# Transposed rows, 512 wide value products, and two reorderings in a three-part transformer layer

## The reference, cut to what matters

```python
x = x + xattn(layernorm(x), ctx)       # x is 256 x 512, ctx 4096 x 512
x = x + ssd(layernorm(x))              # state space block
x = x + experts(layernorm(x))          # 32 routed experts, 6 for a token, and shared ones

# xattn: 16 heads over 4 key/value heads; keys: 4096 of ctx, then the 256 own ones
scores = einsum('blhd,bmhd->bhlm', q, k_full) * scale + mask   # mask: causal on the own keys
out = einsum('bhlm,bmhd->blhd', softmax(scores), v_full) ; out @ wo

# ssd, in 2 chunks of 128 tokens, 16 heads
A_cs = cumsum(dt * A)                                   # over the tokens of a chunk
Lmat = where(tril, exp(A_cs[l] - A_cs[s]), 0)
y = (C B^T * Lmat) @ (x dt) + C @ state * exp(A_cs) + x D
y = rms(y * silu(z)) * norm_weight @ W_out

# experts
s = sigmoid(x @ gate_w); combine = top 6 of s, normed to the sum 1
out = sum_e combine_e * (silu(x wg_e) * (x wu_e)) @ wd_e + shared
```

## Time and profile before

| what | value |
|---|---|
| runs (3) | median 1078.52 us, 1077.47 to 1078.64 |
| the profiled execution | 1078.46 us |
| its span, first to last instruction | 1076.5 us |
| mean granted PE clock | 0.995 |
| busy share PE, DVE, ACT, POOL | 98%, 70%, 52%, 13% |

### The profile page before, as it was taken

How to read it: one execution, slowest core, us unless ns; L and a number is a source line. 1 busy time by engine, 2 the same in 40 slices (tenths; PEclk the granted TensorE clock), 3 DMA queues, 4 the chain that set the end, 5 groups by cost and what they waited for, 6 DMA issues and landing times.

```text
span 1076.5 us, 17012 instructions
## 1 busy us (share of the span) xinstructions
PE 1055.8 (98%) x6685; PEld 939.5 (87%) x6685; DVE 748.7 (70%) x1634; ACT 555.5 (52%) x956; POOL 139.7 (13%) x142
## 2 busy tenths in 40 slices
PE   7999999999999999999999999999999899999998
PEld 6888888878999999999999999999777599999997
DVE  5856777559677777777777777777178667676675
ACT  4434433335766656666655666667035445445442
POOL 4644444330000000000000000004021000000000
PEclk9999999999999999999999999999999899999999
DMA  6758666597004220044002340013520285555550
GB/s 229 253 193 281 199 228 195 167 315 251 1 1 167 81 86 2 1 167 131 37 2 89 118 132 1 1 71 141 227 120 1 81 338 179 181 191 187 181 172 20
DMA packets 64159, 145.85 MB, mean 135 GB/s; under 512 B 3888, under 2 KB 42704, under 8 KB 62672
## 3 DMA queue, kind: packets, MB, share of 16 engines
q1 hardware_dynamic: 64080, 144.77, 39.1%
HBM read 108.55 MB, written 36.21 MB: 134 GB/s over the span
## 4 chain that ended last, share of the span: by engine, by line
PE 92%; DVE 4%; ACT 1%; issue 1%; DMA 0%; POOL 0%; POOLq 0%
PE bank L434 58%; PE bank L453 16%; PE bank L532 11%; PE bank L591 2%; PE bank L463 1%; DVE conv_acc L1026 1%; PE bank L717 1%; PE bank L561 1%; PE bank L604 1%; PE bank L674 1%; PE bank L488 0%; DVE conv_acc L1023 0%; DMA w_ctx_raw<-in_w_ctx 0%; ACT xc L1390 0%; PE bank L635 0%
## 5 line engine op out<-in xcount | busy, mean ns | idle before, releaser
L962 DVE TENSOR_TENSOR pT_lo<-bank,pT_hi 128x512 fp32r<-128x512 f32 x272 | 185.2, 690 | 122.8 <-ACT pT_hi L1357 122.7
L434 PE MATMUL bank<-pT_hi,vN 128*128 128x256 f32 (+1 forms) x1088 | 245.0, 288 | 0.0
L1357 ACT CAST pT_hi<-bank 128x512 fp32r<-128x512 f32 x272 | 159.3, 587 | 161.4 <-PE bank L532 157.0
L434 PEld LDWEIGHTS bank<-pT_hi,vN 128*128 128x128 f32 x1088 | 185.9, 189 | 6.9
L434 PE MATMUL bank<-kT,qT_hi 128*128 128x512 f32 (+2 forms) x576 | 188.5, 408 | 2.1 <-DVE scores L907 2.1
L907 DVE TENSOR_SCALAR_CACHE_REDUCE scores<-bank 128x512 f32<-128x512 f32 x256 | 169.3, 682 | 0.1
L532 PE MATMUL bank<-ident,scores 128*128 128x128 f32 x1072 | 161.4, 272 | 0.9 <-DVE pT_lo L962 0.9
L434 PE MATMUL bank<-fT_hi,e_hl 128*128 128x256 f32 x816 | 156.2, 284 | 0.0
L1328 ACT ACTIVATE scores<-scores,neg_max 128x1024 f32<-128x1024 f32 (+2 forms) x128 | 153.1, 1196 | 5.7 <-DVE neg_max L919 5.7
L434 PE MATMUL bank<-pT_lo,vN 128*128 128x256 f32 (+1 forms) x544 | 153.1, 281 | 0.0
L453 PE MATMUL bank<-w_ctx_hi,ctx_hl 128*128 128x512 f32 x512 | 145.9, 397 | 6.4 <-ACT ctx_hl L1237 6.4
(11 more groups left out here) (201 smaller groups left out, 1349.0 us busy)
## 6 DMA issues: line engine op xcount, KB each, us to landing
e_raw<-in_experts SPq DMA_DIRECT2D x51, 768.0 KB, 4.4
k_spill<-k_stage SPq DMA_DIRECT2D x16, 1024.0 KB, 4.5
v_spill<-v_stage SPq DMA_DIRECT2D x16, 1024.0 KB, 8.6
vN<-v_spill SPq DMA_DIRECT2D x16, 1024.0 KB, 5.2
kT<-k_spill SPq DMA_DIRECT2D x15, 1024.0 KB, 5.3
ctx_raw<-in_ctx SPq DMA_DIRECT2D x15, 512.0 KB, 4.3
w_raw<-in_w_qkv SPq DMA_DIRECT2D x6, 1024.0 KB, 5.1
wo_sb<-in_wo SPq DMA_DIRECT2D x4, 1024.0 KB, 8.6
```

The lines of the kernel that those rows point to most:

```text
L434: done = e.matmul(dst, lhs(a), rhs(w), start=first and m == 0, stop=last and m == 2)
L962: e.tensor_tensor(ring[1][:, :], bank[tb][:, :], ring[0][:, :], ALU.subtract).then_inc(p_lo, 1)
L1357: e.copy(ring[0][:, :], bank[tb][:, :]).then_inc(p_hi, 1)
```

## The change

The reciprocals are spread by two transposes of a broadcast column, straight from `rden`; `diag` goes. The two parts of `pT` stand in one tile, and for a key tile one 512 wide product has V_hi with both parts (V_hi x pT_lo sums in columns 256 to 511 of the bank), and one 256 wide has V_lo x pT_hi. At a head's end DVE copies the upper half, adds the lower, and then multiplies. The decay rows become transposes of a broadcast column of `cs`. `project_z(1, 0)` comes ahead of the triangle product. The second tile's logits follow `up(0)`, the turned `cw` follows `up(1)`, and `up` no longer waits for the plain copy `fT` of the second tile.

```diff
-        pT = [[reg.take(f"pT_hi{i}", [512], F32R), reg.take(f"pT_lo{i}", [512], F32R)] for i, reg in enumerate([region["pt"]] * 3 + [sp_])]
+        pT = [reg.take(f"pT{i}", [2, 512], F32R) for i, reg in enumerate([region["pt"]] * 3 + [sp_])]
...
-                    done = three(bank[5 + z][:, q0:L], lambda v: vN[:, v, kt, :], lambda p: ring[p][:, i * L + q0:(i + 1) * L],
-                                 kt == 0, kt == KTILES - 2)
+                    halves = bank[5 + z][:, :].rearrange("p (a q) -> p a q", a=2)
+                    e.matmul(halves[:, :, q0:L], vN[:, 0, kt, :], ring[:, :, i * L + q0:(i + 1) * L], start=kt == 0, stop=False)
+                    done = e.matmul(halves[:, 0, q0:L], vN[:, 1, kt, :], ring[:, 0, i * L + q0:(i + 1) * L], start=False, stop=kt == KTILES - 2)
...
             def spread_sums(h):
-                pe.wait_ge(inv, 4 * (h + 1))
+                pe.wait_ge(inv, 2 * (h + 1))
-                e.matmul(bank[b][:, 0:L], ones[:, :], diag[h % 2][:, :, :].rearrange("p a b -> p (a b)"), start=True, stop=True).then_inc(spread, 1)
+                for qt in range(2):
+                    done = e.transpose(bank[b][:, qt * P:(qt + 1) * P], rden[h % 2][:, qt, 0:1].to_broadcast([P, P]), ident[:, :])
+                done.then_inc(spread, 1)
...
+            project_z(1, 0)
             pe.wait_ge(dtc, 18)
             e.matmul(bank[5][:, 0:TT * MH], upto[:, :], dA_.rearrange("p t h -> p (t h)"), start=True, stop=True)
             e.matmul(bank[5][:, 64:64 + MH], ones[:, :], dtb[8][:, 0, :], start=True, stop=True).then_inc(dt_mm, 1)
-            project_z(1, 0)
...
             def decay_rows(tt, c, q, bank_sem, bank_count):
-                pe.wait_ge(dtc, 18)
+                pe.wait_ge(cs_done, 1)
-                    done = e.matmul(bank[b][:, i * P:(i + 1) * P], dtb[8][:, tt, h0 + i:h0 + i + 1].to_broadcast([P, P]), upto[:, :], start=True, stop=True)
+                    done = e.transpose(bank[b][:, i * P:(i + 1) * P], cs[:, tt, h0 + i:h0 + i + 1].to_broadcast([P, P]), ident[:, :])
...
-            route_logits(1)
             def up(j):
-                pe.wait_ge(fT_l, 4)
+                pe.wait_ge(fT_l, 3)
...
                 up(j)
                 if j == 0:
+                    route_logits(1)
+                if j == 1:
                     pe.wait_ge(topk, 18)
...
             def invert_sums(h):
-                for qt in range(2):
-                    e.tensor_scalar(diag[z][:, qt, :], ident[:, :], rden[z][:, qt, 0:1], None, ALU.mult).then_inc(inv, 1)
...
             def finish_head(h):
-                e.tensor_tensor(head_out[z][:, :], bank[5 + z][:, 0:L], rden_all[z][:, :], ALU.mult).then_inc(ho, 1)
+                e.tensor_copy(head_out[z][:, :], bank[5 + z][:, L:2 * L]).then_inc(ho_sum, 1)
+                dve.wait_ge(ho_sum, 2 * h + 1)
+                e.tensor_tensor(head_out[z][:, :], bank[5 + z][:, 0:L], head_out[z][:, :], ALU.add).then_inc(ho_sum, 1)
+                dve.wait_ge(ho_sum, 2 * h + 2)
+                e.tensor_tensor(head_out[z][:, :], head_out[z][:, :], rden_all[z][:, :], ALU.mult).then_inc(ho, 1)
```

More of the change, by code:

```diff
@@ L280, in build_program @@
         rden = [sp_.take(f"rden{i}", [2, 1]) for i in range(2)]
-        diag = [sp_.take(f"diag{i}", [2, P]) for i in range(2)]
         rden_all = [sp_.take(f"rden_all{i}", [2 * P]) for i in range(2)]
@@ L374, in build_program @@
         p_hi, p_lo, pv, inv, spread, rden_done = sem("p_hi"), sem("p_lo"), sem("pv"), sem("inv"), sem("spread"), sem("rden_done")
+        ho_sum = sem("ho_sum")
         ho, oT_hi, oT_lo = sem("ho"), sem("oT_hi"), sem("oT_lo")
@@ L924, in invert_sums @@
                 e.reduce_sum(den[z][:, :, 0], sums[z][:, :, :], AX).then_inc(inv, 1)
-                dve.wait_ge(inv, 4 * h + 1)
+                dve.wait_ge(inv, 2 * h + 1)
                 e.reciprocal(rden[z][:, :, 0], den[z][:, :, 0]).then_inc(inv, 1)
-                dve.wait_ge(inv, 4 * h + 2)
-                for qt in range(2):
-                    e.tensor_scalar(diag[z][:, qt, :], ident[:, :], rden[z][:, qt, 0:1], None, ALU.mult).then_inc(inv, 1)
             def finish_head(h):
@@ L961, in dve_program @@
                     tb, ring = (3, 4, 7)[n % 3], pT[n % NPT]
-                    e.tensor_tensor(ring[1][:, :], bank[tb][:, :], ring[0][:, :], ALU.subtract).then_inc(p_lo, 1)
+                    e.tensor_tensor(ring[:, 1, :], bank[tb][:, :], ring[:, 0, :], ALU.subtract).then_inc(p_lo, 1)
                     for s in plan.in_step[h, kk]:
@@ L1356, in act_program @@
                             act.wait_ge(v_out[slot], 16 * NBATCH // 2)
-                    e.copy(ring[0][:, :], bank[tb][:, :]).then_inc(p_hi, 1)
+                    e.copy(ring[:, 0, :], bank[tb][:, :]).then_inc(p_hi, 1)
                     for p in plan.parts_in_step[h, kk]:
```

## The result

The changed kernel took 1070.12 us (median of 4 runs, 1069.87 to 1071.55), the kernel before, run beside it, 1078.58 us. The ratio is 0.9921, 95% interval 0.9909 to 0.9933. The same kernel run again gave 1069.65 us, ratio 0.9921 (0.9908 to 0.9933). So 8.5 us went, where 6.85 were forecast.

What follows compares the result with a forecast made beforehand. TensorE (PE) bounds attention, VectorE (DVE) the state space stretch. Attention -8.7, state space -0.15, clock +1.2 and expert entry +0.8 sum to -6.85 us: 1078.5 to 1071.7 us, own range 1070.5 to 1073.4, whole range 1068.4 to 1075.0.

Steps and rivals of the forecast that it cites:

- The last pair: Attention, each head's last two key tiles, odd one masked for 128 queries: 0.69 to 0.583 us, 0.107 saved, 1.7 in all.
- the spread: Attention, denominators' rows: two transposes at 0.22 us replace a full-precision product at 0.43, saving 0.21 x 16 = 3.4 us.
- 512 x 0.007 = 3.6 us: Attention, wide value product: each of 512 key tiles saves 2 x 0.120 - 0.233 = 0.007 us of PE.
- rival B: Attention: the wide value product saves nothing, as equal columns suggest; 1075.3 us, chance 0.13.
- C: Attention: the wide value product runs at 0.227 us, like the context projection's products; 1068.6 us, chance 0.11.
- The missing diagonals give nothing: Last head of attention: dropping two diagonal builds on DVE gains 0, since pT_lo there waits for ACT's cast.
- Cost nothing: Attention, head's end on DVE: head_out 0.85 to 0.9 us later, absorbed in two to three steps; uncovered 14.4 us.
- at least 3.4 us of cover: Attention, head's end: PE uses the delayed pT_lo three steps later, steps taking 1.16 to 2.56 us.
- The hole: State space part: PE's 1.63 us softplus idling, filled by the z product, only moves to 806.8 to 808.4; worth nothing.
- The clock near 811: State space part: PE, thinned to 2.6 of 6.1 us, falls to half clock for some 7 us, costing 1.2 us.
- rival A: State space part: the clock holds because transposes keep PE busy enough; 1070.5 us, chance 0.24.
- Entry of the experts: Start of the expert part: reordered logits make tile 2 start at 862.55, not 861.8; 0.8 us lost, 0.45 at full clock.

## Why the prediction was right, and where not

- **Attention, forecast 8.7, measured 7.85.** The last pair (0.106 a head) and the spread (0.21 a head) came as worked out; between the landmarks each counts in 15 heads, 1.6 and 3.2 us. The mis-sized term is "512 x 0.007 = 3.6 us": by the steps it is 4.5 ns a tile, 2.3 us. The step that failed is the pricing of a 256 wide product at 0.120 us, and with it of a tile's saving, from pieces rounded to 0.01 us. The Trainium skill, "TensorE: Matmul & The Clock Gate", section "Back-to-back issue gap", has a formula for a single warm matmul, N/2.4 ns plus 2.5, from which an estimate of 2.5 ns a merged pair follows, 1.3 us. The measured 2.3 lies between that and the forecast. Neither rival B (nothing) nor C (13 ns) holds.
- **"The missing diagonals give nothing": wrong by 1.2 us.** In the last head pT_lo waited for DVE as well, and not for ACT's cast alone. Three steps of it are 1.23 us longer in the trace before than in the one after, and 1.57 longer with the diagonals back in the changed kernel.
- **The head's end, "Cost nothing": right where score chunks run beside it, for the wrong reason, and wrong in the last head.** The step that failed is "at least 3.4 us of cover". It followed the delay through pT_lo alone. What comes first is the score eviction behind pT_lo, whose bank PE wants: 0.4 us are left after the change, by an estimate 1.3 before it with the 0.9 that the change took. A delay begins to cost from there, not from 3.4. In the last head nothing covers it, and the longer end costs 0.55 us. So the sum for attention is 2.3 + 1.6 + 3.2 + 1.2 - 0.55 = 7.75 of the 7.85.
- **State space part: 0.14 us measured, 0.15 forecast.** The hole moved, as told: PE of the changed kernel waits 1.75 us for ACT at 800.26. That the totals agree is in part luck: the decay rows alone are worth 0.36 us by the trace with them put back, so the rest of this part lost some 0.2.
- **The clock near 811, forecast 1.2 us: not in the changed kernel's trace.** The stretch thinned as forecast and the clock held at 1.00; this is rival A, and the nearest to the measured time. With the spread undone it fell in that very stretch, for 3.4 us and 0.8 us of path. The step that failed is to read one busy share ahead of one fall as what decides. (In its working, 812.91 and twice 1.88 us make 816.7, not 816.3.)
- **Entry of the experts, forecast 0.8 lost, measured 0.3 gained.** At the same clock at the entry the reordering does lose about 1 us (its undoing gives 0.98). What came on top is the half clock, 6.8 us in the trace after and 10.2 in the one before; the forecast took it as given. Whether the new order shortened it or chance did is not settled: undone, the trace has 6.8 us too, but the clock of the runs is lower. The late transfer of weights was covered, as forecast: ACT idled for 5.5 us once, 3.3 more than its usual 2.2, and PE's only waits for e_hl are the 0.5 us ahead of tile 2. Waits, 845 to 1060 us:

```profile
ACT e_hl L1440 <- PE bank L435: 95.1, 44, 2.5
...
ACT e_hl L1440 <- DMA e_raw<-in_experts: 5.5, 1, 5.5
PE bank L435 <- DVE e_hl L1136: 0.5, 1, 0.5
```

- **Sum.** -7.85 - 0.14 - 0.26, and the 0.37 us from ahead of attention, where nothing was changed: -8.6 by the trace. Against the forecast, attention gave 0.85 too little, clock and entry 1.2 and 1.1 more than counted. That the total came near owes something to luck, to errors of both signs.

## What to carry to other kernels

- Cover on a queue is not the lag of the product that reads the delayed tile. Go through each instruction queued behind, ask which buffer it frees and when that is wanted again; the smallest of these is the cover. Dependent copies put in at the place measure it; take several doses, and read the length of the step and not the listed wait, which left out 0.27 us here.
- Price small differences between PE shapes from many instructions (the starts of steps over many heads), not from pieces rounded to 0.01 us: 7 ns a tile were forecast, 4.5 measured.
- Look at the last round of a loop by itself. Work that covers a delay in every other round is missing there: the last head alone held 1.2 us of gain and 0.55 us of cost that the forecast put at nothing.
- Where PE idles for some microseconds ahead of dense work, useless products or transposes in the waits can pay: 1.0 to 1.7 us here at one place.

## What was unexpected of the hardware

- The stretches at half clock are not the same from one kernel's trace to another's where the code is alike: they begin near 242, at 802 or 808.8, or between 840.8 and 849.7 us (in the kernels of 1065 to 1077 us), and last 3.4, 6.8 or 10.2 us. The mean granted clock of one kernel's runs goes from 0.991 to 0.998, and the time from 1071.8 down to 1067.7 us.
- Useless transposes alone (20 in 2.38 us, 14 in 1.69 us) kept the clock at 1.00 where PE's idling had let it fall.
- A fall of the clock for 3.4 us in the attention costs 1.5 us.
- PE lost 0.27 us more in a step than the list of waits shows, after a wait of 0.71 us as after one of 2.09.
